# A slot table over one and a quarter batches in the Mamba stage of a one-core hybrid block

## The reference, cut to what matters

```python
xz = x @ in_proj_w.T                 # 256 -> 1024
xc, z = jnp.split(xz, 2, axis=-1)    # 512 channels each
h = causal convolution of xc, 4 taps, 512 -> 512 channels, plus conv_b
u = h
dt = jnp.clip(jax.nn.sigmoid(u @ dt_w.T + dt_b), 0.0001, 1.0)
A = -jnp.exp(A_log)                  # 512 x 16
Bm = u @ B_w.T ;  Cm = u @ C_w.T     # 16 states
def step(state, inp):
    dA = jnp.exp(jnp.clip(dtt[:, :, None] * A, -5.0, 5.0))
    dB = dtt[:, :, None] * bt[:, None, :] * ut[:, :, None]
    state = dA * state + dB + 1e-06
    y = jnp.sum(state * ct[:, None, :], axis=-1) + D * ut
y = y * jax.nn.silu(z)
return y @ out_w.T
```

## Time and profile before

| | us |
|---|---|
| median of 3 runs (1835.03, 1840.58, 1847.00) | 1840.58 |
| the profiled execution, time of the run | 1838.69 |
| the profiled execution, span | 1836.60 |
| Mamba stage, first scan to the end of POOL's work | 958.3 |

### The profile page before, as it was taken

The page is one execution under the profiler, slowest core; times in us unless marked ns, Lnnn a source line. Parts: engine busy times, 40 slices in busy tenths (PEclk is TensorE's granted clock), DMA queues, the critical chain, the costliest instruction groups (busy, mean ns, idle before and its releaser), DMA issues.

```text
span 1836.6 us, 21675 instructions
## 1 busy us (share of the span) xinstructions
PE 1511.0 (82%) x6374; PEld 943.0 (51%) x6375; DVE 1148.3 (63%) x1762; ACT 967.1 (53%) x1749; POOL 1032.1 (56%) x354
## 2 busy tenths in 40 slices
PE   2899686999687979979889899898997872809997
PEld 1566572666443545545456455455554542805665
DVE  4566530444433798788888888878888985303443
ACT  1222111333225888788888787877877870103332
POOL 2111005122101999989899898998998995061222
PEclk9999867999998999999999999999998796559999
DMA  9800105122210111111111111111110111422110
GB/s 319 295 0 0 35 25 160 46 57 61 82 42 6 35 36 39 35 34 37 35 36 35 36 37 39 34 37 35 36 37 34 41 35 60 158 93 64 60 58 24
DMA packets 67888, 108.61 MB, mean 59 GB/s; under 512 B 8729, under 2 KB 37278, under 8 KB 67552
## 3 DMA queue, kind: packets, MB, share of 16 engines
q1 hardware_dynamic: 54240, 76.65, 14.0%
q0 software_dynamic: 9344, 27.31, 4.0%
q10 hardware_dynamic: 4224, 3.67, 0.6%
HBM read 80.04 MB, written 29.39 MB: 60 GB/s over the span
## 4 chain that ended last, share of the span: by engine, by line
PE 68%; DVE 10%; POOL 9%; issue 6%; ACT 3%; DMA 2%; ACTq 1%; SPq 1%; DVEq 0%; POOLq 0%
PE ps L1026 13%; PE ps L1249 12%; PE ps L1186 8%; PE ps L1169 7%; POOL arena L372 5%; PE ps L1281 5%; DVE arena L982 4%; PE ps L1354 3%; PE ps L1051 3%; PE ps L1333 3%; PE ps L1221 2%; POOL arena L379 2%; PE ps L1147 2%; PE ps L1313 2%; PE ps L1088 2%
## 5 line engine op out<-in xcount | busy, mean ns | idle before, releaser
L982 DVE TENSOR_TENSOR_SCAN arena<-arena,ps 128x512 f32<-128x512 f32 x512 | 617.3, 1214 | 154.0 <-PE ps L1026 141.5
L372 POOL TENSOR_TENSOR arena<-arena 128x2048 f32<-128x2048 f32 x128 | 580.8, 4542 | 160.0 <-DVE arena L982 160.0
L1026 PEld LDWEIGHTS ps<-cst,arena 128*128 128x128 f32 x2836 | 365.7, 150 | 421.1 <-issue 282.2
L1026 PE MATMUL ps<-cst,arena 128*128 128x128 f32 x2836 | 461.9, 290 | 139.5 <-DVE arena L831 51.6
L558 ACT ACTIVATE arena<-arena,a_neg 128x512 f32<-128x512 f32 x512 | 366.8, 717 | 119.7 <-DVE arena L982 119.1
L568 ACT ACTIVATE arena<-arena,m_bt 128x512 f32<-128x512 f32 x512 | 362.9, 709 | 16.3 <-PE ps L1026 16.1
L379 POOL TENSOR_TENSOR arena<-arena 128x2048 f32<-128x2048 f32 x64 | 290.5, 4539 | 5.0
L1249 PE MATMUL ps<-arena,tapw 128*128 128x512 f32 x512 | 250.3, 607 | 0.0
L479 ACT ACTIVATE arena<-ps,b1t 128x128 f32<-128x128 f32 x312 | 88.9, 368 | 167.2 <-PE ps L1026 167.2
L347 POOL DMA_INDIRECT sorted_rows<-x,pos x64 | 62.2, 972 | 195.8 <-DVE tile_e L816 176.9
L1186 PE MATMUL ps<-arena 128*128 x624 | 151.3, 385 | 7.5 <-ACT arena L479 2.9
(11 more groups left out here) (132 smaller groups left out, 1469.8 us busy)
## 6 DMA issues: line engine op xcount, KB each, us to landing
arena<-c_rows SPq DMA_DIRECT2D x128, 256.0 KB, 3.3
arena<-in_W SPq DMA_DIRECT2D x32, 512.0 KB, 10.6
sorted_rows<-arena POOLq DMA_DIRECT2D x2, 5070.0 KB, 36.3
arena<-sorted_rows SPq DMA_DIRECT2D x78, 130.0 KB, 2.1
x<-in_x SPq DMA_DIRECT2D x8, 512.0 KB, 10.8
arena<-in_conv SPq DMA_DIRECT2D x4, 1024.0 KB, 6.5
x<-residual SPq DMA_DIRECT2D x8, 512.0 KB, 8.1
arena<-in_b SPq DMA_DIRECT2D x2, 1024.0 KB, 11.7
```

The source lines that it names most:

```text
L372: g.tensor_tensor(h, h, m_c[i % RC].unsqueeze(1).to_broadcast([P, KI, SEQ]), ALU.mult)\
L982: v.tensor_tensor_scan(out=h[:, k, :], data0=m_a[g % RA], data1=ps[2 + g % 2][:, :], initial=0.0, op0=ALU.mult, op1=ALU.add).then_inc(S("m ...
L1026: return t.transpose(bank, src[:, k * P:(k + 1) * P], ident)
```

## The change

The table now spans one and a quarter batches. The x turn (slots 48, 49) and the first two of the four output groups of the convolution (slots 50 to 61), with their copies and the first u turn, are issued for batch b+2 in batch b (`m_early`); the other two groups come in slots 0 to 12 of batch b+1. Batch 1 is an exception: its whole convolution stays in batch 0 (`FIRST_...`). B and C move to 14 to 16, dt to 22 to 44 and into bank 1 alone, z to 32 to 46 and bank 0 alone, output to 18 to 28 and bank 0 (both halves), the updates of x to 20 and 28, and the four row statistics into slots 29 to 32, one each. Waits at the first calls follow the new sharing of the banks. What is computed is the same.

```diff
--- before.py
+++ after.py
@@ -49,39 +49,47 @@
 PAIRS, PE_PAIRS = NS // 2, 3
 NSUM_AT = 17
-CONV_AT = ((0, 0, 1, 2, 2, 3, 4, 4), (5, 6, 6, 7, 8, 8, 9, 10), (10, 11, 12, 12, 13, 14, 14, 15),
-           (16, 16, 18, 18, 20, 20, 22, 22))
-UT_AT = (7, 13, 19, 25)
-OUT_AT = ((24, 24, 24, 24, 26, 26, 26, 26), (36, 36, 36, 36, 38, 38, 38, 38))
-BC_AT = (28, 28, 30, 30)
-DT_AT = ((32, 32, 34, 34), (40, 40, 41, 42), (46, 46, 47, 48), (52, 52, 53, 54))
-DTT_AT = (38, 45, 51, 57)
-BT_AT = 40
-Z_AT = ((42, 43), (48, 49), (54, 55), (58, 58))
-XT_AT = (60, 62)
-UC_AT = (5, 11, 16, 23)
-UTC_AT = (8, 14, 20, 26)
-BCC_AT = 31
-TH_AT = (35, 43, 49, 55)
-ZTH_AT = (44, 50, 56, 59)
-NORM_AT = (46, 47, 52, 53)
-XTC_AT = (61, 63)
+XT_AT = (48, 49)
+CONV_AT = ((50, 51, 52, 52, 53, 54, 55, 55), (56, 57, 57, 58, 59, 59, 60, 61), (0, 0, 1, 2, 2, 3, 4, 5),
+           (6, 7, 7, 8, 9, 10, 11, 12))
+FIRST_CONV_AT = ((0, 0, 0, 0, 1, 1, 1, 1), (2, 2, 2, 2, 3, 3, 3, 3), (5, 5, 5, 5, 6, 6, 6, 6),
+                 (8, 8, 9, 9, 10, 10, 11, 12))
+UT_AT = (61, 2, 8, 14)
+FIRST_UT_AT = (4, 6, 9, 14)
+BC_AT = (14, 14, 15, 16)
+OUT_AT = ((18, 18, 18, 18, 20, 20, 20, 20), (26, 26, 26, 26, 28, 28, 28, 28))
+DT_AT = ((22, 22, 24, 24), (30, 30, 31, 32), (36, 36, 37, 38), (42, 42, 43, 44))
+DTT_AT = (27, 35, 41, 47)
+BT_AT = 30
+Z_AT = ((32, 33), (37, 38), (41, 43), (45, 46))
+XTC_AT = (49, 50)
+UC_AT = (56, 62, 6, 13)
+FIRST_UC_AT = (2, 4, 7, 13)
+UTC_AT = (62, 3, 9, 15)
+FIRST_UTC_AT = (5, 7, 10, 15)
+BCC_AT = 17
+TH_AT = (25, 33, 39, 45)
+ZTH_AT = (34, 39, 44, 47)
+NORM_AT = (41, 42, 43, 44)
 ADD_AT = 20
 FINAL_AT = (14, 15, 16, 17)
-UPDATE_AT = (27, 39)
+UPDATE_AT = (20, 28)
+STAT_AT = (29, 30, 31, 32)
 SKIP_AT = (34, 36, 38, 40)
-CLIP_AT = (36, 44, 50, 56)
-WT_AT = (39, 46, 52, 58)
-BTC_AT = 41
-GATE_AT = (45, 51, 57, 60)
-XT_BANK, CONV_BANK, UT_BANK, OUT_BANK = (0, 1), (0, 1, 0, 1), (0, 1, 0, 1), (0, 1)
-BC_BANK, BT_BANK, DT_BANK, DTT_BANK, Z_BANK = 1, 1, (0, 0, 1, 0), (0, 0, 1, 0), (1, 0, 1, 1)
+CLIP_AT = (25, 33, 39, 45)
+WT_AT = (27, 35, 41, 47)
+BTC_AT = 30
+GATE_AT = (34, 39, 44, 47)
+XT_BANK, CONV_BANK, UT_BANK, OUT_BANK = (1, 0), (1, 0, 1, 0), (1, 0, 1, 0), (0, 0)
+BC_BANK, BT_BANK, DT_BANK, DTT_BANK, Z_BANK = 1, 0, (1, 1, 1, 1), (1, 1, 1, 1), (0, 0, 0, 0)
 AT_BANKS = ((6, 0, 3), (7, 3, 3), (1, 6, 2))
@@ -568,28 +576,40 @@
                 a.activation(m_dbt[i % 2][:, c, :], m_wt[b % 2][:, c, :], ACT.Copy, bias=1e-6,
                              scale=m_bt[b % 2][:, c, n:n + 1]).then_inc(S("m_dbt"), 1)
+            def m_early(n, q):
+                for k in range(KD):
+                    if q == XTC_AT[k]:
+                        m_xtcopy(n, k)
+                for o in range(2):
+                    if n != 1 and q == UC_AT[o]:
+                        m_uevac(n, o)
+                if n != 1 and q == UTC_AT[0]:
+                    m_utevac(n, 0)
             def m_pre(n, q):
-                if q in UC_AT:
-                    m_uevac(n, UC_AT.index(q))
-                if q in UTC_AT:
-                    m_utevac(n, UTC_AT.index(q))
+                for o in range(KI):
+                    if q == (FIRST_UC_AT if n == 1 else UC_AT)[o] and (n == 1 or o >= 2):
+                        m_uevac(n, o)
+                    if q == (FIRST_UTC_AT if n == 1 else UTC_AT)[o] and (n == 1 or o >= 1):
+                        m_utevac(n, o)
                 if q == BCC_AT:
                     m_bchi(n)
                 if q in TH_AT:
                     m_thevac(n, TH_AT.index(q))
                 if n < BATCH - 1 and q in NORM_AT:
                     m_norm(n + 1, NORM_AT.index(q))
-                if n < BATCH - 1 and q in XTC_AT:
-                    m_xtcopy(n + 1, XTC_AT.index(q))
+                if n < BATCH - 1:
+                    m_early(n + 1, q)
             a.wait_ge(S("m_zero"), 2)
             a.wait_ge(S("m_stat0"), 1)
             a.wait_ge(S("m_aexp"), 3)
             for c in range(CPB):
                 m_norm(0, c)
-            for k in range(KD):
-                m_xtcopy(0, k)
+            for q in range(SLOTS):
+                m_early(0, q)
             for q in range(SLOTS):
                 m_pre(0, q)
             for g in range(AHEAD):
@@ -947,12 +967,12 @@
                 xv = x[:, c:c + 2, :]
                 v.tensor_tensor(xv, ps[bank][:, :].rearrange("p (c d) -> p c d", c=2), xv, ALU.add)\
                     .then_inc(S("m_xupd"), 1)
-                if h == 0:
-                    return
+            def m_stat(b, c):
                 v.wait_ge(S("m_xupd"), 2 * b + 2)
-                for c in range(CPB):
-                    last = row_stats(CPB * b + c)
-                last.then_inc(S("m_stat"), 1)
+                last = row_stats(CPB * b + c)
+                if c == CPB - 1:
+                    last.then_inc(S("m_stat"), 1)
             def m_pre(n, q):
@@ -997,6 +1017,8 @@
                             m_final(b - 1, FINAL_AT.index(q))
                         if b and q in UPDATE_AT:
                             m_update(b - 1, UPDATE_AT.index(q), OUT_BANK[UPDATE_AT.index(q)])
+                        if b and q in STAT_AT:
+                            m_stat(b - 1, STAT_AT.index(q))
                         if q in GATE_AT:
                             m_gate(b, GATE_AT.index(q))
@@ -1016,6 +1038,8 @@
                 m_final(BATCH - 1, k)
             m_update(BATCH - 1, 0, 0)
             m_update(BATCH - 1, 1, 1)
+            for c in range(CPB):
+                m_stat(BATCH - 1, c)
             feed(1, "m_stat", BATCH)
@@ -1259,25 +1283,18 @@
             def m_bcmm(n, k):
                 if k == 0:
-                    t.wait_ge(S("m_utc"), KI * (n + 1))
+                    t.wait_ge(S("m_utc"), KI * n + 3)
+                    t.wait_ge(S("m_u"), KI * (n + 1))
                 mm = t.matmul(ps[BC_BANK][0:2 * NS, :], bcw[:, k, :], m_u[n % 2][:, k, :], start=(k == 0), stop=(k == KI - 1))
                 if k == KI - 1:
                     mm.then_inc(S("m_bcmm"), 1)
             def m_dtmm(n, o, k):
                 if k == 0:
-                    if o == 0 and n >= 2:
-                        t.wait_ge(S("m_xupd"), 2 * (n - 2) + 1)
-                    if o == 1:
-                        t.wait_ge(S("m_wt"), KI * n + 1)
-                    if o == 2 and n:
-                        t.wait_ge(S("m_sz"), KI * (n - 1) + 1)
-                    if o == 2 and n == 0:
-                        t.wait_ge(S("m_btc"), 1)
-                    if o == 3 and n:
-                        t.wait_ge(S("m_sz"), KI * (n - 1) + 2)
-                    if o == 3 and n == 0:
-                        t.wait_ge(S("m_wt"), 2)
+                    if o == 0:
+                        t.wait_ge(S("m_bchi"), n + 1)
+                    else:
+                        t.wait_ge(S("m_wt"), KI * n + o)
                 mm = t.matmul(ps[DT_BANK[o]][:, :], dtw[:, k, o * P:(o + 1) * P], m_u[n % 2][:, k, :],
                               start=(k == 0), stop=(k == KI - 1))
                 if k == KI - 1:
@@ -1287,6 +1304,8 @@
                 t.wait_ge(S("m_bchi"), n + 1)
                 if n >= 2:
                     t.wait_ge(S("m_xupd"), 2 * (n - 1))
+                else:
+                    t.wait_ge(S("m_utc"), KI * (n + 1))
                 for c in range(CPB):
                     last = t.transpose(ps[BT_BANK][:, c * P:c * P + 2 * NS], m_bc[0:2 * NS, c * P:(c + 1) * P],
                                        ident[0:2 * NS, 0:2 * NS])
@@ -1300,16 +1319,13 @@
             def m_zmm(b, o, k):
-                end = b == BATCH - 1
-                if k == 0:
-                    if o == 0:
-                        t.wait_ge(S("m_xupd" if end else "m_btc"), 2 * b if end else b + 2)
-                    if o == 1:
-                        t.wait_ge(S("m_xupd" if end else "m_wt"), 2 * b - 1 if end else KI * (b + 1) + 2)
-                    if o == 2:
-                        t.wait_ge(S("m_sz" if end else "m_wt"), KI * b + 1 if end else KI * (b + 1) + 3)
-                    if o == 3:
-                        t.wait_ge(S("m_sz"), KI * b + 3)
+                if k == 0 and o == 0:
+                    if b == BATCH - 1:
+                        t.wait_ge(S("m_xupd"), 2 * b)
+                    else:
+                        t.wait_ge(S("m_btc"), b + 2)
+                elif k == 0:
+                    t.wait_ge(S("m_sz"), KI * b + o)
                 mm = t.matmul(ps[Z_BANK[o]][:, :], zw[:, k, o * P:(o + 1) * P], m_xt[b % 2][:, k, PAD:],
                               start=(k == 0), stop=(k == KD - 1))
                 if k == KD - 1:
@@ -1320,17 +1336,14 @@
                 if i == 0:
                     t.wait_ge(S("m_y"), KI * (b + 1))
                     if h == 0 and b < BATCH - 2:
-                        t.wait_ge(S("m_utc"), KI * (b + 2) + 3)
-                    if h == 0 and b == BATCH - 2:
-                        t.wait_ge(S("m_wt"), KI * BATCH)
-                    if h == 1 and b < BATCH - 2:
```

(48 more changed lines are left out.)

## The result

The changed kernel takes 1852.74 us (median of 8 runs, 1851.75 to 1860.47), the kernel before 1845.62 (8 runs, 1835.03 to 1847.57). The ratio is 1.0054, 95% interval 1.0031 to 1.0076 (the two medians alone give 1.0039): slower by about half a per cent, where 4.9 us faster was forecast. It lies inside the range for the time (1803 to 1856) and within the 1% called "same", but the sign is wrong.

A forecast was written before the change was run, and what follows sets the result against it. Order of work, not engine sums, bounds it: 116.1 us walk, 0.3 restarts, 1.1 clock make period 117.5. Stage 950.4 against 958.3, prologue +3.0: 4.9 us faster, 1836 allowing for the runs' median; range 1803 to 1856.

The forecast's parts named there:

- The walk: New table followed slot by slot with measured pitches and handover prices, each engine in program order: 116.1 us a batch.
- the five stretches: Slots 24 to 31, 32 to 47, 48 to 63, 0 to 15, 16 to 23: 15.6+35.7+25.2+25.5+14.1 us.
- the clock term: TensorE partly at 1.2 instead of 2.4 GHz after idle stretches: nothing to 3.4 us a batch, 1.1 taken.
- T=33 to 38: Microseconds after slot 32's spread: TensorE idle stretches where VectorE leads, so a slow stretch is nearly hidden.
- 87 to 90.6: Microseconds after slot 32's spread: output matmuls stand on the chain, half clock costs up to 1.7 us.
- the slower rival: Half clock follows waits at 36 and 42 (and 18) every batch: period 119.8, time 1852; 18 in 100.
- the signs named for being wrong: Period under 114, dt matmuls without a wait, convolution delaying VectorE to slot 63, half clock every batch at 36 to 44.
- its restarts: TensorE restarting after a wait, 0.1 us each: three on the chain, 0.3 us a batch.
- batch 0: Batch 1's whole and half of batch 2's convolution fall into it: 63.5 us to scan 32, 99.2 to slot 48.
- the prologue: Before the stage: dt groups 2 and 3 later 1.8 us, third convolution group 1.2; together +3.0 us.
- The backlog cap: Rival: POOL's backlog capped at slot 17; gains over 4.5 us stop TensorE; period 118.5, 1842 us; 6 in 100.
- the hidden chain: Rival: waits at 36 and 42 lie beside other work; period near 112.5, 1806 us; 12 near 1805, 8 to 1781.

The follow-up runs named there:

- the second experiment: Changed kernel plus two matmul calls with unused result in the wait ahead of dt group 2 (slot 36): 1845.68 us, ratio 1.0023.
- the second profile: Profile of the changed kernel run once more, unaltered, for its prologue: 1856.40 us.
- The best version: Changed kernel with earlier transposes, weighing and finals, two D u additions moved, and batch 1's first half convolution in the prologue: 1805.47 us, ratio 0.9802.
- one bank alone: Kernel before with only the bank sharing: all dt groups in bank 0, all z groups in bank 1, slots as they were: 1898.11 us, ratio 1.0291.
- the kernel with no half ahead: Changed kernel with every batch's convolution in slots 0 to 12 of the batch before it, as batch 1's: 1940.40 us, ratio 1.0528.
- the first experiment: Changed kernel with transposes and weighing of dt groups 1, 2 and 3 one slot earlier (34, 40, 46): 1830.30 us, ratio 0.9941.

## Why the prediction was wrong

The walk, by its own steps. From the first scan to the end of POOL's work 950.4 us were forecast; it is 964.3 (587.93 to 1552.21).

- *Right:* the bound. No engine's sum counted but the order of work, and slots 32 to 47 carried it. The walk gave 15.6, 35.7, 25.2, 25.5 and 14.1 us for the five stretches; the profile has 15.7, 37.6, 25.7 to 26.4, 25.9 and 14.2. Both waits at the dt bank are there at 1.9 and 1.5 us, and the wait of the output matmuls for the last final at 1.63 (forecast 1.9).
- *The step that failed: the clock term.* "From nothing to 3.4 us a batch; I take 1.1", with the slow stretches placed at T=33 to 38, where they would be nearly hidden, and 87 to 90.6. At 87 to 90.6 (slot 18) the clock never fell in the changed kernel. At T=33 to 38, behind the 2.26 us wait ahead of the x turns, it fell in batches 0, 1, 2 and 4, at 0.5 to 0.8 us each. And it fell where the walk had none: behind the wait before dt group 2, in each of batches 1 to 6, on the chain, worth 1.7 us by the second experiment. That is the mechanism I had set aside under the slower rival ("z, dt and sums refill TensorE between the waits") and one of the signs named for being wrong. Over the six cycles from slot 48 of batch 0 this is 2.1 us each where 1.1 was taken.
- *The walk itself was short too.* With the clock up the five stretches add up to 117.4, as the second experiment's best batches show, where the walk and its restarts gave 116.4. Clock and walk share the miss about equally: the six cycles took 717.4 us (119.6 each) instead of 705: +12.4. The stated point from which the change loses, a period of 118.3, was passed.
- *Sized too small: batch 0.* To slot 48 it takes 103.6 us instead of 100.1, +3.5. All of it lies ahead of slot 32. The walk left out that the third convolution group waits 1.17 us for the copy of a u turn, and gave 1.7 us to the slow start; how the rest divides is not shown.
- *Sized too small: the prologue.* +3.0 forecast, +5.8 in the first profile and +10.5 in the second: the handovers are as forecast, but the clock fell on dt group 2 (5.4 us for 3.6), and in the second profile on group 3 too (6.3), behind the new waits for the weighing.
- *Not of the change:* the stage's first transposes began 2.0 us later in the profile (508.75 against 506.73); over all profiles that moment lies between 503.7 and 509.8.
- *Right:* the end; from slot 48 of batch 6 to POOL's last addition 143.3 us for 145.3.

Together 2.8 + 2.0 + 3.5 + 12.4 - 2.0, and 0.3 behind POOL's end, make the 19.0 us between the forecast of 4.9 us less and the profile's 14.1 more.

Of the rivals, the slower one had the right mechanism; that its 1852 and its period of 119.8 were hit is in part luck, for it counted two falls on the chain in every batch, and one of them, with the walk's own shortfall and a part of another fall, made the same sum. The backlog cap did not act in the middle batches: TensorE waits for POOL once in the stage's batches 1 to 7, for 1.25 us in batch 7, and every shortening of the chain shortened the period. The best version reaches the period of 112.5 that was named for the hidden chain; the change as made had the chain in the open.

## What to carry to other kernels

When buffers are pooled by use (one bank for dt, one for z) instead of rotated, the way back of the buffer becomes part of the loop: give the release its place in the table before the next user, a slot ahead if the engines lead one another by slots. In a loop of short handovers walk the order with measured pitches; the sums of the engines will not show it. And price a wait on the TensorE chain with what follows it: here 1.9 us of idle cost 3.6 in six of seven batches.

## What was not expected of the hardware

A wait as short as 1.9 us (changed kernel), or of 3.5 us (one bank alone), was followed by half clock on the very matmuls that had been waited for. But the length of that wait does not decide it. The same 1.89 us before dt group 2 left the clock up in batch 0, and in batches 0 and 2 to 6 of the kernel with no half ahead. The 2.26 us ahead of the x turns was followed by half clock in batches 0, 1, 2 and 4 and not in 3 and 5 (in the repeat of the same kernel in 0, 1, 3 and 4); the 1.48 us before group 3 never was; and in the first experiment 1.63 us before the output matmuls was, in batches 2 and 6 alone. Matmuls in place of the 1.89 us kept the clock at its full level. And the fall of the clock is not fixed by the program: one and the same prologue took 79.2 and 83.9 us in two executions, with the same instructions at 3.71 and 6.30 us. A difference under 5 us between kernels with such a prologue should be read from the periods, not from one time.
